# One-hots of the relation types made by POOL, a group at a time between its gathers, in place of VectorE

## The reference, cut to what matters

```python
x, y, c = h[src], h[dst], w_comp[etype]              # etype: one of 86 relations
msg = einsum('eb,ebo->eo', c, einsum('ei,bio->ebo', x, weight))   # 16 bases
x_hat = x @ A1_w.T + A1_b
y_hat = y @ A2_w.T + A2_b + rel_emb[etype]
a = tanh(relu(sum(x_hat * y_hat, -1) / sqrt(32)))
nei = segment_sum(a[:, None] * msg, dst)
```

## Time and profile before

| | |
|---|---|
| timed runs | 17,230.35 us median of 3 (17,207.27 to 17,251.48) |
| profiled execution | span 17,231.0 us; no work lies outside it |
| mean granted TensorE clock | 0.617 of full speed |
| busy, whole span | PE 37%, PEld 23%, DVE 41%, ACT 16%, POOL 55% |
| relation pass | 10,955 to 14,098 us of the span |
| granted clock in the pass | 0.84 |

### The profile page before, as it was taken

One profiled execution on the slowest core, in us unless ns is written; L12 is line 12 of the kernel. 1 busy time (PEld: TensorE's weight loads), 2 busy tenths in 40 slices (PEclk: granted clock), 3 DMA queues, 4 the chain that ended last, 5 costly groups with the idle time before them and its releaser, 6 DMA issues. The chain is left out here.

```text
span 17231.0 us, 133710 instructions
## 1 busy us (share of the span) xinstructions
PE 6403.2 (37%) x28658; PEld 4040.9 (23%) x28659; DVE 7021.0 (41%) x15685; ACT 2781.2 (16%) x4350; POOL 9553.7 (55%) x9902
## 2 busy tenths in 40 slices
PE   4212222444444112212122222466566656344446
PEld 1111111222222111111011111222222226232234
DVE  6322222222222233333366667666666652232232
ACT  1112212444444111111000001000000001000001
POOL 0566666555555666664666664355454551666663
PEclk9555555666666555555555555688888875666665
DMA  2111111222221111112233332222222222111111
GB/s 88 25 24 26 25 25 40 62 60 61 60 61 49 18 19 19 19 19 83 70 86 88 88 87 73 49 56 57 55 57 55 57 59 56 19 20 20 19 20 47
DMA packets 761665, 826.94 MB, mean 48 GB/s; under 512 B 353366, under 2 KB 526785, under 8 KB 758438
## 3 DMA queue, kind: packets, MB, share of 16 engines
q0 software_dynamic: 340624, 383.65, 12.0%
q1 hardware_dynamic: 271806, 297.17, 5.7%
q10 hardware_dynamic: 148312, 136.41, 2.8%
HBM read 657.66 MB, written 158.81 MB: 47 GB/s over the span
## 5 line engine op out<-in xcount | busy, mean ns | idle before, releaser
L736 POOL DMA_INDIRECT rel_ring<-scratch_tab,k_src x1664 | 1583.0, 951 | 1557.0 <-DVE rel_message L2281 1033.7
L675 PE MATMUL rel_accumulator<-rel_message,rel_onehot 128*128 128x512 f32 x3328 | 1762.1, 678 | 1203.1 <-DVE rel_message L2281 968.4
L1229 POOL DMA_INDIRECT sum0g_ring<-scratch_parts,k_group_src x1568 | 1558.7, 994 | 1098.5 <-issue 479.7
L1229 POOL DMA_INDIRECT sum1g_ring<-scratch_parts,k_group_src x1568 | 1531.9, 977 | 1122.0 <-SPq L1243 622.0
L736 POOL DMA_INDIRECT pass_ring<-scratch_tab,k_src x1664 | 1654.6, 994 | 867.4 <-issue 486.1
L736 POOL DMA_INDIRECT sh_ring<-scratch_tab,k_src x1664 | 1569.9, 943 | 939.2 <-issue 495.7
L1229 POOL DMA_INDIRECT sum2g_ring<-scratch_parts,k_group_src x1568 | 1518.4, 968 | 933.6 <-issue 466.2
L675 PE MATMUL sh_accumulator<-sh_message,sh_onehot 128*128 128x248 f32 x3328 | 1055.1, 446 | 1444.8 <-issue 1407.7
L675 PEld LDWEIGHTS sh_accumulator<-sh_message,sh_onehot 128*128 128x128 f32 x3328 | 750.2, 228 | 1749.1 <-issue 1681.3
L675 PEld LDWEIGHTS rel_accumulator<-rel_message,rel_onehot 128*128 128x128 f32 x3328 | 684.1, 217 | 1991.7 <-issue 1991.6
L2281 DVE TENSOR_TENSOR rel_message<-numbers,rel_ring 128x2048 f32<-128x2048 f32 x416 | 953.0, 2291 | 14.3
(11 more groups left out here) (435 smaller groups left out, 14437.8 us busy)
## 6 DMA issues: line engine op xcount, KB each, us to landing
rel_rel_rows<-scratch_rel_rows ACTq DMA_DIRECT2D x211, 256.0 KB
pass_rows<-scratch_rel_rows SPq DMA_DIRECT2D x208, 256.0 KB
scratch_kv<-pass_ring SPq DMA_DIRECT2D x208, 256.0 KB
pass_kept<-scratch_kv SPq DMA_DIRECT2D x208, 256.0 KB
rel_type_rows<-scratch_type_rows ACTq DMA_DIRECT2D x211, 172.0 KB
rel_ring<-scratch_tab,k_src POOLq DMA_INDIRECT x1672
pass_ring<-scratch_tab,k_src POOLq DMA_INDIRECT x1664
sh_ring<-scratch_tab,k_src POOLq DMA_INDIRECT x1664
```

Source lines behind the costliest of these rows:

```text
L675: self.nc.tensor.matmul(self.accumulator[:, bass.ds(self.banks[g], self.width)], onehot, rows, start=False, stop=True, skip_group_check=Tr ...
L736: nc.gpsimd.indirect_dma_start(out=ring[:, q, g, :], out_offset=None, in_=table, in_offset=bass.IndirectOffsetOnAxis(ap=k["src"][:, n * G ...
L1229: nc.gpsimd.indirect_dma_start(out=ring[:, n % slots, g, :], out_offset=None, in_=table, in_offset=bass.IndirectOffsetOnAxis(ap=k["group_s ...
```

## The change

POOL makes `kind_t`, for a whole group (86x1024) at once, at the head of each batch of gathers. `kind_t` has three buffers of a group in place of two of a half group; the space comes from one of the four `message` buffers, which now lies in `hat`, a tensor that is not used during the pass. POOL waits for the row loads of the group and, from the fourth group on, for the look-ups of three groups earlier. VectorE and TensorE wait for the new semaphore `kinds`.

```diff
-        kind_t = [sb(f"kind_t{m}", [N_REL, H, P], BF16) for m in range(2)]
+        kind_t = [sb(f"kind_t{m}", [N_REL, G, P], BF16) for m in range(3)]
...
-        message = [sb(f"message{m}", [P, H, WIDTH]) for m in range(4)]
+        message = [sb(f"message{m}", [P, H, WIDTH]) for m in range(4 - len(lent))]
+        message += [a[:].rearrange("p j f -> p (j f)")[:, 0:H * WIDTH].rearrange("p (g w) -> p g w", g=H) for a in lent]
...
             _one_hot(nc, k, onehot[m], n * H, H)
-            _one_hot_of_rows(nc, k, onehot_t[m % 2][:].rearrange("p g e -> p (g e)"), rel_rows[:, m // 2, half])
-            _one_hot_of_rows(nc, k, kind_t[m % 2][:].rearrange("p g e -> p (g e)"), type_rows[:, m // 2, half]).then_inc(made, 1)
+            if n % 2 == 0 and n >= 2:
+                dve.wait_ge(kinds, n // 2)
+            _one_hot_of_rows(nc, k, onehot_t[m % 2][:].rearrange("p g e -> p (g e)"), rel_rows[:, m // 2, half]).then_inc(made, 1)
+
+        def make_kinds(pool, u):
+
+            pool.wait_ge(rowed[u % R], (u // R + 1) * 2 * DMA)
+            if u >= 3:
+                pool.wait_ge(looked_up, 2 * (u - 2))
+            nc.gpsimd.tensor_scalar(kind_t[u % 3][:].rearrange("p g e -> p (g e)"), type_rows[:, u % R, :],
+                                    k["step_no"][0:N_REL, 0:1], None, ALU.is_equal).then_inc(kinds, 1)
...
+            if n % 2 == 0:
+                pe.wait_ge(kinds, n // 2 + 1)
             for g in range(H):
-                nc.tensor.matmul(looked[:, m % 2, g, 0:3 * LOOK], kind_t[m % 2][:, g, :], relations[:], start=True, stop=True)
+                nc.tensor.matmul(looked[:, m % 2, g, 0:3 * LOOK], kind_t[n // 2 % 3][:, n % 2 * H + g, :], relations[:], start=True, stop=True)
...
-                _gather_rows(nc, pool, k, dram["tab64"][0:J * P, :], ring, R, gathered,
-                             lambda n, q: pool.wait_ge(messaged, n * 2 + 1))
-
-                pool.wait_ge(messaged, GROUPS * 2 + 1)
+                def between(n, q):
+                    pool.wait_ge(messaged, n * 2 + 1)
+                    make_kinds(pool, n)
+
+                _gather_rows(nc, pool, k, dram["tab64"][0:J * P, :], ring, R, gathered, between)
+
+                for n in (GROUPS, GROUPS + 1):
+                    pool.wait_ge(messaged, n * 2 + 1)
+                    make_kinds(pool, n)
```

More of the change, by code:

```diff
@@ L2214, in gather_last_sources, with relation_pass @@
     pool.wait_ge(own, J * DMA)
-def relation_pass(nc, k, dram, y_nodes, relations, node_split):
+def relation_pass(nc, k, dram, y_nodes, relations, node_split, lent=()):
     H, WIDTH, LOOK = G // 2, N_BASES * D, D + N_BASES
@@ L2246, in relation_pass @@
         gathered = [sem(f"gathered{q}") for q in range(R)]
-        saved, split = sem("saved"), sem("split")
+        saved, split, kinds = sem("saved"), sem("split"), sem("kinds")
         def load_rows_of(act, group, slot):
@@ L2421, in relational @@
                       + split_steps(v, lambda c: relations[:, 3 * D + c * N_BASES:3 * D + (c + 1) * N_BASES], table_rest[:, D:LOOK], table[:, D:LOOK])
-                      + [lambda: v.memset(current[:], 0.0)])
+                      + [lambda: v.memset(current[:], 0.0)], lent=(hat,))
         with ExitStack() as inner:
```

## The result

| | before | after |
|---|---|---|
| median of the timed runs | 17,226.7 us | 16,794.3 us (16,776 to 16,819, 4 runs) |
| ratio | | 0.9744, 95% interval 0.973 to 0.9758 |
| profiled execution | 17,231.0 us | 16,779.5 us |
| relation pass, a group | 15.0 us | 12.9 us |

The group is the time from the first to the last multiplication for the logits, by 208 (before: from the first to the last message, by 207.5). It went from 15.0 to 12.9 us; 208 x 2.1 = 437 us of the 451 us between the two profiles lie there.

A forecast was written before the change was run, and what follows sets the result against it. Back-to-back gathers were taken to bound the relation pass. POOL's 11.8 us plus 1.1 of remaining stalls gave 12.9 us a group against 15.0: 208 x 2.1 = 437 us off 17,231, so 16,794 us, range 16,420 to 17,400.

The forecast's parts named there:

- What bounds the stage: Relation pass: no engine is full; VectorE stalls 12 to 13 us behind back-to-back batches of POOL's gathers.
- The first rival: Relation pass: stalls stay, tied to POOL working at all; only VectorE's 108 us are saved, 17,123 us; chance 0.13.
- VectorE's saving: One TENSOR_SCALAR less in each half group on VectorE: 0.52 us a group, 9.8 becomes 9.3.
- POOL's operation: New 86x1024 TENSOR_SCALAR at the head of POOL's batch: 1.7 us, making POOL's group 11.8 us, the longest.
- What is left of stalls: VectorE in the relation pass: a stall of 5 to 7 us every fifth group, 1.1 us a group.
- The contention: POOL's operation holds up VectorE's short bf16 one-hots: at most 1.3 us a group, covered by POOL's 11.8 us.
- The wait for the rows: POOL waits for its group's row loads: a batch waiting for release starts 3 to 8 us later, opening the distance.
- slower: Relation pass: stalls stay while operation and row wait lengthen POOL's turn, 16.2 us a group, 17,480 us; chance 0.2.
- nothing: Relation pass: POOL's added turn eats VectorE's saving, cycle of three groups stays, 17,231 within 52 us; chance 0.07.

The follow-up runs named there:

- f3: Kernel before plus a POOL comparison of 86x1024, result unread, ahead of each batch of gathers, on a chip with stalls: 16,808.8 us, ratio 0.9768.
- g1: Kernel before without VectorE's one-hots of types from the third half group on, nothing new on POOL, on a chip with stalls: 17,180.6 us, ratio 1.0008.
- e1: Kernel before plus a POOL comparison of 86x1024, result unread, ahead of each batch of gathers, on a chip without stalls: 14,530.9 us, ratio 1.0398.
- f4: Kernel before plus a POOL comparison of 86x512, result unread, ahead of each batch of gathers, on a chip with stalls: 16,690.5 us, ratio 0.9704.
- e3: Kernel before with POOL also waiting for the row loads of its group ahead of each batch, on a chip without stalls: 14,052.2 us, ratio 1.0053.
- f1: Kernel before, unchanged, run again for its profile on a chip with stalls: 17,211.7 us.
- g2: Kernel before plus a POOL comparison of 86x256, result unread, ahead of each batch of gathers, on a chip with stalls: 17,037.4 us, ratio 0.9937.
- g3: Kernel before plus two unread POOL comparisons of 86x256 a group, ahead of the batch and after its fourth gather, chip with stalls: 16,563.0 us, ratio 0.9646.
- first set: The first four follow-up kernels, all on one chip without the stalls, where the kernel before took 13,974 us.
- e2: Kernel before without VectorE's one-hots of types from the third half group on, nothing new on POOL, on a chip without stalls: 13,930.6 us, ratio 0.9969.
- e4: Changed kernel with POOL's comparison made twice a group, on a chip without stalls: 15,161.1 us, ratio 1.0846 to the kernel before.

## Why the prediction was right, by its own steps

- **What bounds the stage: right, and shown.** Back-to-back gathers, not an engine. f3 gives VectorE no relief and gets the whole gain; g1 gives it the whole relief and gets nothing. The first rival (VectorE's saving alone, 17,123) falls with g1: even its 108 us did not come. Its condition, that the stalls are tied to POOL working at all, falls with f3, where POOL works more and they are gone.
- **VectorE's saving: 0 us of the time.** 0.52 us a group were saved on VectorE, hidden behind POOL, which the sum had right by counting POOL's group only.
- **POOL's operation: mis-sized.** 1.7 us were taken, 0.94 to 2.3 the bounds; it measured 2.87. The COPY of 128 elements scaled up was no upper bound. The three sizes that ran give 0.98, 1.59 and 2.87 us for 256, 512 and 1024 columns: about 0.35 us and 2.5 ns a column. "GPSIMD Engine Reference" of the Trainium skill, Performance versus the Vector engine, has 1.8 cycles an element at best and about 2.6 for a two-input operation, by estimates from that page 1.5 and 2.2 us; the measured 2.87 us of this one-input comparison lie above both.
- **What is left of stalls: mis-sized the other way.** 1.1 us a group were added for it. None of it came on top of POOL's own turn: 10.02 + 2.87 = 12.89 us, and the stage took 12.9. VectorE's 2.8 us a group ahead of its one-hots lay inside that turn. Part of them is the effect: f3 stands there for 474 us in all, e1, the same kernel on the chip without stalls, for 181. In f4, whose turn is 11.6 us, 0.8 us of such stalls show. The two errors, +1.2 and -1.1, cancelled; it was luck that the sum of 12.9 us and the total of 16,794 were hit so closely.
- **The contention: real, and covered.** VectorE's `onehot_t` took 507 ns on average in the changed kernel, against 360 before, and up to 1.8 us: 0.3 us a group, within the 1.3 allowed and under POOL's 12.9.
- **The wait for the rows: not seen.** It was to cost 3 to 8 us for a batch that waits for its release. With POOL's queue as the bound no batch waits for a release any more, and the rows are there: the waits of POOL on them sum to 3.4 us. That the wait opens the distance was part of the argument and isn't shown; nothing in the result needs it.
- **The rivals "slower" and "nothing"** priced mechanisms that did not occur: an operation that doesn't count as a rest from gathers, and a cycle of three groups that stays. But the change does lose where the stalls are absent: e1, the same load on POOL, is 1.04 on such a chip, and by its POOL work the changed kernel would be there too; it was not run there. The prediction took the chip for granted and had no rival for this. It was right for the chip that it was made and measured on.

## What to carry to other kernels

Look for what stalls have in common beyond the releaser's name: here the names were wrong, and only the timelines of POOL and VectorE side by side gave the rule. Where VectorE and ScalarE stall late in a long run of indirect DMAs, break the run: a short POOL operation every four gathers, its result unused, gained 3.5%, more than the change (2.4 to 2.6%). Measure such a cure on more than one chip first: a comparison of 86x1024 a group costs 4% where there is nothing to cure.

## What the runs showed of the hardware that was not expected

- One kernel, unchanged, took 13,974 us on one chip and 17,168 to 17,227 on three others or at three other times, 23% apart, with the runs on each within 0.4%. The kernel before has no profile from the fast chip, but e3 differs by one wait. The relation pass takes 3,136 us in f1 and 2,211 in e3, and 906 of these 925 us are idle time of VectorE: the stalls behind gathers in a row. Of the 3,160 us between the two profiles 1,715 more lie ahead of the pass and 520 behind it. No run tried the cure in those stages.
- On a chip with the effect it builds up over a run of gathers: runs of eight with 0.4 us between them stall VectorE for 13 us, with 1.2 us for 6 us on average, with 3 us for 3.5 at most ahead of its one-hots; runs of four with 1.15 us between them hardly. ScalarE's issues slow down with it (2.12 us in place of 0.44 between two loads), and the longest stalls end about 3 us after the last gather of the run.
- The slow thing is not only a transfer. ScalarE and SyncE run some 4,550 register and branch instructions in the pass, which touch no tensor; ScalarE's ALU_OP takes 38 ns as a rule. In the kernel before, 197 of them take over 0.5 us, most of these 0.70 (f1: 165), and 116 of the 197 fall into VectorE's 48 idle times of over 9 us. In g2 155 do, in f4 116, in the changed kernel 82, in g3 20, and on the chip of the first set not one, in e1, e2, e3 or e4. So these instructions tell a chip with the effect from one without, and how much of it is left. Which part of the chip is shared, and why some chips show it and others don't, no run here tells.
